# Lower triangles of 2048 Gram matrices on one core: laps of two tiles turned by halves, and stores of neighbouring batches as one run

## What is computed

```python
# inputs: (2048, 64, 256), float32
Z = jnp.einsum('bnd,bmd->bnm', inputs, inputs)
li, lj = jnp.tril_indices(64, k=-1)
y = Z[:, li, lj]
```

## Time and profile before

| | us |
|---|---|
| median of three runs (lowest to highest) | 401.72 (401.25 to 402.3) |
| the profiled execution, its own time | 403.43 |
| its span, first to last instruction | 401.6 |
| busy in the span: PE, DVE | 365.2, 362.3 |
| busy in the span: ACT, POOL | 178.4, 197.7 |
| DMA | 151.01 MB, 376 GB/s on average |

### The profile page before, as it was taken

How to read it: one execution, slowest core, us unless ns; L and a number is a source line. 1 busy time by engine, 2 the same in 40 slices (tenths; PEclk the granted TensorE clock), 3 DMA queues, 4 the chain that set the end, 5 groups by cost and what they waited for, 6 DMA issues and landing times.

```text
span 401.6 us, 68674 instructions
## 1 busy us (share of the span) xinstructions
PE 365.2 (91%) x33024; PEld 359.8 (90%) x33024; DVE 362.3 (90%) x240; ACT 178.4 (44%) x821; POOL 197.7 (49%) x974
## 2 busy tenths in 40 slices
PE   4439999999999999999999999998999899998960
PEld 4439999999999999999999999998989899998960
DVE  3417899999999999999999998989999798998995
ACT  0011224555445544465445654453554344455463
POOL 1000047282833866086817475283835738184585
PEclk9999999999999999999999999999999999999995
DMA  8299999999999999999999999999999999998417
GB/s 319 105 351 427 420 422 423 420 405 421 422 425 402 422 425 421 422 415 425 420 424 413 421 417 419 352 399 417 381 425 360 425 370 422 403 366 339 138 31 206
DMA packets 21274, 151.01 MB, mean 376 GB/s; under 512 B 2688, under 2 KB 2816, under 8 KB 4864
## 3 DMA queue, kind: packets, MB, share of 16 engines
q1 hardware_dynamic: 18752, 135.77, 83.8%
q10 hardware_dynamic: 2496, 14.97, 9.6%
HBM read 134.22 MB, written 16.52 MB: 375 GB/s over the span
## 4 chain that ended last, share of the span: by engine, by line
DVE 43%; DMA 34%; issue 13%; PE 8%; DVEq 0%
DVE x_turned L233 38%; DMA x_in<-x_dram 34%; PE bank_set L311 8%; DVE row_halves L250 3%; DVE x_in L257 1%; DVE packed_rows L153 1%; DVE packed_rows L142 0%; DVE x_turned L262 0%; DVEq L249 0%; DVEq L232 0%; DVEq L74 0%; DVEq L282 0%
## 5 line engine op out<-in xcount | busy, mean ns | idle before, releaser
L311 PE MATMUL bank_set<-x_turned 32*64 32x64 f32 x33024 | 365.2, 237 | 23.3 <-issue 15.1
L311 PEld LDWEIGHTS bank_set<-x_turned 32*64 32x64 f32 x33024 | 359.8, 132 | 28.5 <-issue 16.1
L233 DVE STREAM_TRANSPOSE x_turned<-x_in 128x2048 f32<-128x2048 f32 x128 | 287.9, 2280 | 33.8 <-PE bank_set L311 18.4
L153 POOL COPY packed_rows<-row_halves 32x32 f32<-32x32 f32 (+30 forms) x930 | 190.0, 204 | 198.3 <-DVE row_halves L250 98.6
L342 ACT COPY products<-bank_set 128x512 f32<-128x512 f32 (+1 forms) x91 | 68.4, 758 | 153.1 <-PE bank_set L311 141.0
L250 DVE STREAM_TRANSPOSE row_halves<-products 128x1024 f32<-128x1024 f32 x60 | 72.2, 1205 | 0.0
L142 ACT COPY packed_rows<-row_halves 128x32 f32<-128x32 f32 (+30 forms) x465 | 61.4, 220 | 16.6 <-DVE row_halves L250 16.5
L148 ACT COPY packed_rows<-row_halves 128x128 f32<-128x128 f32 x240 | 54.0, 299 | 27.8 <-DMA y_dram<-packed_rows 16.1
L342 ACT ACT_TABLE_LOAD x1 | 1.3, 1283 | 19.6 <-PE bank_set L311 19.6
L153 POOL COPY packed_rows<-x_in 32x32 f32<-32x32 f32 (+30 forms) x31 | 4.9, 209 | 0.1
L257 DVE STREAM_TRANSPOSE x_in<-products 128x512 f32<-128x512 f32 (+1 forms) x5 | 4.8, 998 | 0.0
## 6 DMA issues: line engine op xcount, KB each, us to landing
x_in<-x_dram SPq DMA_DIRECT2D x128, 1024.0 KB, 16.2
y_dram<-packed_rows ACTq DMA_DIRECT2D x22, 504.0 KB, 9.2
y_dram<-packed_rows ACTq DMA_DIRECT2D x6, 252.0 KB
y_dram<-packed_rows ACTq DMA_DIRECT2D x24, 63.0 KB
y_dram<-packed_rows SPq DMA_DIRECT2D x2, 504.0 KB, 4.7
y_dram<-packed_rows SPq DMA_DIRECT2D x1, 380.0 KB
y_dram<-packed_rows ACTq DMA_DIRECT2D x1, 380.0 KB
y_dram<-packed_rows SPq DMA_DIRECT2D x1, 124.0 KB
```

What stands on the lines that cost most here:

```text
L153: return copy(packed_rows[first:first + BLOCK, group % 2, :, at + BLOCK:at + i], halves(group)[first + BLOCK:first + HALF, i, :, 0:i - BLOCK])
L233: nc.vector.transpose(x_turned[:, j].rearrange("p c b s (h u n v) -> p u v (c b s h) n", h=ROWS // BLOCK, u=PAIRS, v=PAIR), x_in[:, k]).th ...
L311: done = nc.tensor.matmul(bank_sets[s][side * HALF:(side + 1) * HALF, g, at, :].rearrange("r (n u v) -> r u n v", u=PAIRS, v=PAIR), rows, ...
```

## The change

- The lap has two tiles instead of three, so 64 laps hold 128 tiles and the blank tile goes. x_turned has room for two tiles, and each PSUM set takes one.
- Each tile is turned and multiplied in two halves (PARTIALS), each of four of the eight chunks: DVE runs two transposes of 1024 elements a tile instead of one of 2048, with a semaphore for each place and half; PE waits for each half; a half's place is free once PE is done with that half. PE's order in a half is slot, then chunk; `start` is given once for a bank, at the first slot's first chunk.
- ACT keeps each tile by itself, 128 copies of 512 elements. They are written in another order, so that the two batches of a partition in packed_rows are neighbours in y: a run of 16128 bytes for each partition. For the last group the order stays as it was within each run, and SP and ACT store it in twice as many DMAs (HALF_SIDES), 16 partitions each.
- Small DMAs only in groups 1, 5 and 9 instead of 1, 3, 5, 7, 9 and 11: 12 instead of 24.
- Only load 4 is held, until PE is done with tile 0. Load 5 is not.
- PACK_LAG is 20 quarters instead of 19, counted against tiles instead of sets.

```diff
-    LAP = 3
-    LAPS = -(-TILES // LAP)
-    BLANK = LAPS * LAP - TILES
-    SET_TILES = (2, 1)
-    SETS = len(SET_TILES)
+    LAP = 2
+    LAPS = TILES // LAP
+    SETS = LAP
+    PARTIALS = 2
+    PARTIAL = CHUNKS // PARTIALS
...
-    PACK_LAG = 2 * PIECE_LAG - 3
+    PACK_LAG = 2 * PIECE_LAG - 2
...
+    HALF_SIDES = [[(side, q, q + BLOCK // SLOTS) for q in range(0, BLOCK, BLOCK // SLOTS)] for side in range(SIDES)]
...
-        x_turned = sbuf("x_turned", [PARTS, LAP, CHUNKS, SLOTS, SIDES, ROWS])
+        x_turned = sbuf("x_turned", [PARTS, LAP, CHUNKS, SIDES, SLOTS, ROWS])
...
+        def wait_kept(engine, t):
+            lap, s = place(t)
+            engine.wait_ge(kept[s], (lap + 2) * LAP)
...
         def by_few(group):
-            return group % 2 == 1 and group <= FEW_UNTIL
+            return group % 4 == 1 and group <= FEW_UNTIL
...
         def store(engine, group, columns, lanes):
-            rows = y[group * GROUP:(group + 1) * GROUP, columns].rearrange("(h q s) c -> s q h c", h=RUNS, s=SIDES)
+            rows = y[group * GROUP:(group + 1) * GROUP, columns]
             for side, first, end in lanes:
-                engine.dma_start(rows[side, first:end],
-                                 packed_rows[side * HALF + first:side * HALF + end, group % 2, :, columns]).then_inc(
-                    stored[group % 2], 16)
+                packed = packed_rows[side * HALF + first:side * HALF + end, group % 2, :, columns]
+                if group < GROUPS - 1:
+                    to = rows.rearrange("(q s h) c -> s q h c", s=SIDES, h=RUNS)[side, first:end]
+                else:
+                    to = rows.rearrange("(h q s b) c -> s b q h c", h=RUNS, s=SIDES, b=SLOTS)[side, first * SLOTS // BLOCK]
+                engine.dma_start(to, packed).then_inc(stored[group % 2], 16)
...
                 if t >= IN_RING:
                     lap, j = place(t - IN_RING)
-                    sync.wait_ge(turned[j], (lap + 1) * LAP)
+                    sync.wait_ge(turned[j][PARTIALS - 1], (lap + 1) * LAP)
                 elif t == LATE:
                     lap, j = place(0)
-                    sync.wait_ge(tile_multiplied[j], lap + 1)
-                elif t == LATE + 1:
-                    lap, j = place(0)
-                    sync.wait_ge(kept[set_of(j)[0]], (lap + 2) * LAP)
+                    sync.wait_ge(multiplied[j][PARTIALS - 1], lap + 1)
...
                 dve.wait_ge(loaded[k], (t // IN_RING + 1) * 16)
-                if lap > 0:
-                    dve.wait_ge(tile_multiplied[j], lap)
-                nc.vector.transpose(
-                    x_turned[:, j].rearrange("p c b s (h u n v) -> p u v (c b s h) n", h=ROWS // BLOCK, u=PAIRS, v=PAIR),
-                    x_in[:, k]).then_inc(turned[j], LAP)
+                for h in range(PARTIALS):
+                    chunks = slice(h * PARTIAL, (h + 1) * PARTIAL)
+                    if lap > 0:
+                        dve.wait_ge(multiplied[j][h], lap)
+                    nc.vector.transpose(
+                        x_turned[:, j, chunks].rearrange(
+                            "p c s b (h u n v) -> p u v (c s b h) n", h=ROWS // BLOCK, u=PAIRS, v=PAIR),
+                        x_in[:, k].rearrange("p (r d) -> p r d", r=JOINED)[
+                            :, :, chunks.start * BLOCK:chunks.stop * BLOCK]).then_inc(turned[j][h], LAP)
...
+                for h in range(PARTIALS):
+                    pe.wait_ge(turned[j][h], count)
+                    for slot in range(SLOTS):
+                        last_slot = h == PARTIALS - 1 and slot == SLOTS - 1
+                        if j == LAP - 1 and last_slot:
+                            pe.reg_add(count, count, LAP)
+                        for c in range(h * PARTIAL, (h + 1) * PARTIAL):
+                            if last_slot and c == CHUNKS - 2:
+                                pe.wait_ge(kept[1 - j], count)
...
+                                        start=c == 0 and slot == 0, stop=c == CHUNKS - 1 and slot == SLOTS - 1)
+                    done.then_inc(multiplied[j][h], 1)
...
+            def keep(t):
+                lap, s = place(t)
+                group, in_group = divmod(t, GROUP_TILES)
+                act.wait_ge(multiplied[s][PARTIALS - 1], lap + 1)
+                if group >= KEPT_RING and in_group == 0:
+                    act.wait_ge(rows_turned, (group - KEPT_RING + 1) * PIECES)
+                to = products[:, group % KEPT_RING]
+                if group < GROUPS - 1:
+                    to = to.rearrange("p i (b t g) -> p i t g b", b=RUNS, g=QUADRANTS)
+                else:
+                    to = to.rearrange("p i (r b t g) -> p r i t g b", r=RUNS, b=SLOTS, g=QUADRANTS)[
+                        :, in_group // (GROUP_TILES // RUNS)]
+                nc.scalar.copy(to[:, :, in_group % to.shape[2]], bank_sets[s][:, :, 0:SLOTS, :].rearrange("p g b i -> p i g b")).then_inc(
+                    kept[s], LAP)
...
-                    while n + PACK_LAG < (lap * LAP + (SET_TILES[0] if s == 0 else LAP) - BLANK) * 2:
+                while n + PACK_LAG < 2 * (t + 1):
```

More of the change, by code:

```diff
@@ L196, in _ @@
             for b in range(2):
-                last = 2 * len(WHOLE_SIDES) * 16 if (GROUPS - 1) % 2 == b else 0
+                last = 2 * sum(map(len, HALF_SIDES)) * 16 if (GROUPS - 1) % 2 == b else 0
                 sync.wait_ge(stored[b], stores_before(GROUPS + b) + last)
@@ L240, in turn_rows @@
                 if piece == 0:
-                    lap, j = place((group + 1) * GROUP_TILES - 1)
-                    s = set_of(j)[0]
-                    dve.wait_ge(kept[s], (lap + 2) * LAP)
+                    wait_kept(dve, (group + 1) * GROUP_TILES - 1)
                 if group > 0:
@@ L329, in _ @@
         def _(act):
-            def keep(lap, s):
-                j = SET_TILES[0] * s
-                act.wait_ge(tile_multiplied[j + SET_TILES[s] - 1], lap + 1)
-                begin = lap * LAP + j - BLANK
-                t, end = max(0, begin), begin + SET_TILES[s]
-                while t < end:
-                    group, in_group = divmod(t, GROUP_TILES)
-                    count = min(end - t, GROUP_TILES - in_group)
-                    if group >= KEPT_RING and in_group == 0:
-                        act.wait_ge(rows_turned, (group - KEPT_RING + 1) * PIECES)
-                    last = nc.scalar.copy(
-                        products[:, group % KEPT_RING, :, in_group * PER_SIDE:(in_group + count) * PER_SIDE].rearrange(
-                            "p i (m g b) -> p i m g b", g=QUADRANTS, b=SLOTS),
-                        bank_sets[s][:, :, (t - begin) * SLOTS:(t - begin + count) * SLOTS, :].rearrange(
-                            "p g (m b) i -> p i m g b", b=SLOTS))
-                    t += count
-                last.then_inc(kept[s], LAP)
+            def keep(t):
[12 more added lines that the diff above has]
+                    kept[s], LAP)
             def pack(n):
@@ L374, in _ @@
             few = 0
-            for lap in range(LAPS):
-                for s in range(SETS):
-                    keep(lap, s)
-                    if n >= (stores + 1) * PIECES * 4:
-                        store_whole(stores)
-                        stores += 1
-                        few = len(FEW_LANES) if by_few(stores - 1) else 0
-                    elif few > 0:
-                        store(act, stores - 1, slice(0, PACKED), FEW_LANES[-few:][:1])
-                        few -= 1
-                    while n + PACK_LAG < (lap * LAP + (SET_TILES[0] if s == 0 else LAP) - BLANK) * 2:
-                        pack(n)
-                        n += 1
+            for t in range(TILES):
+                keep(t)
+                if n >= (stores + 1) * PIECES * 4:
+                    store_whole(stores)
+                    stores += 1
+                    few = len(FEW_LANES) if by_few(stores - 1) else 0
+                elif few > 0:
+                    store(act, stores - 1, slice(0, PACKED), FEW_LANES[-few:][:1])
+                    few -= 1
+                while n + PACK_LAG < 2 * (t + 1):
+                    pack(n)
+                    n += 1
             for n in range(n, LAST_HOME):
```

47 lines of the change are left out of this document (14 added, 33 removed).

## The result

The changed kernel takes 409.17 us (median of 6 runs, 407.16 to 412.62) against 402.04 before (6 runs, 401.25 to 403.02): a ratio of 1.019, with a 95% interval of 1.014 to 1.024. The forecast was 394.7, with a range up to 400.0. The profiled execution took 407.16 us, its span is 405.4. One run of one kernel further down (the sevens) fell into a slower state of the chip, and its ratio and difference leave that run out.

What follows compares the result with a forecast made beforehand. PE and DVE were taken as equal bounds until about 240 us, then late loads. Start -3.7, load waits -9.5, pace +5.8, ends and rounding +0.4 gave 394.7 us, range 391.0 to 400.0.

Steps and rivals of the forecast that it cites:

- Fewer small stores: Stores, 12 small ones instead of 24: four engines' lag falls from 12 to 6 us, loads about 9.7 sooner with the start.
- the waits of 9.5 us: DVE's waits for loads after about 240 us: all go, -9.5 us, with 2 to 3 us to spare.
- near 4 of 16: End of the loads: a DMA share of 0.20 taken as four engines, those of the small stores, behind the rest.
- The start's gain: First lap: tile 0 ends and load 4 goes out one piece of code sooner, -3.7 us.
- the sum: Whole kernel: start -3.7, waits on loads -9.5, pace +5.8, ends and rounding +0.4; span 394.6 us, time 394.7.
- The first lap: Start: no blank tile and less code to wait for; load 4 and PE 3.7 us sooner, bounds 0 and 6.
- PE's pace: PE's laps: branching spread over two tiles instead of three, 2.76 becomes 2.79 us a tile.
- the turns by halves: DVE's transposes: two of 1024 add 0.055 us a tile; cycle 5.62 us for two tiles, DVE becomes the bound.
- A pair of batches as one run: Stores to y: same bytes, packets may double in size; at most 1.4 us, taken as 0.
- ACT: ACT's copies and issues: copies of 583 ns have room; four last-group DMAs instead of two cost +0.3 us on the path.
- the loads stay the bound: Rival, after 240 us: half of the 9.5 us stays, 399.5 us; if all, 404; chance 12%.
- dearer halves: Rival, DVE's turns: halves cost 131 ns a tile, not 55; cycle 5.77, time 403.4 us; chance 8%.

Runs made afterwards that it cites:

- the sevens: Kernel before, last 16 partitions of the second side stored as 7, 7 and 2 in nine groups: 18.1 us more, ratio 1.045.
- short stores: First 14 groups store only 128 of 2016 columns, rest of output left out: 393.07 us for the kernel before, 398.02 changed, against 402.77.
- eights: Kernel before, last 16 partitions of the second side stored as 8 and 8 in each of the first 14 groups: 426.04 us, ratio 1.060.
- sixes: Kernel before, last 16 partitions of the second side stored as 6, 6 and 4 in nine groups: 420.08 us, ratio 1.045.
- both parts taken back: Changed kernel with single runs, whole sides at the end and small stores in six groups again: 401.57 us against 401.88, ratio 0.9987.

## Why the prediction was wrong

The step that failed is *Fewer small stores*: "the lag of 12 us falls to 6. With the start, loads are about 9.7 us sooner at the end." The four engines did carry the small stores and did lag, by 8 us at the last load, and in the changed kernel this lag is gone. But they were not the last. One further engine was 3.8 us behind them, and the small stores were its relief: a group with them puts 6 runs on it instead of 8. With three such groups fewer it has 6 runs more, 3.2 us at 0.53 us each, and putting them back is worth 3.8 us. I read a share of 0.20 as "near 4 of 16" and did not ask who is last among those that are late; the stretch behind it, 377 to 380, held a store that hid it.

The same step had the waits of 9.5 us go. With short stores they do go, by 9.7 us, so their size and their cause in transfers were right. In the real run 7.7 of them stay in the window of the earlier trace rows and one more of 1.35 us stands before the last tile. The start's gain was not lost on PE: load 4 landed at 20.2 us instead of 24.5. It was the slow engine's chain that did not become shorter. From load 4 to load 127 it takes 363.5 us instead of 356.2. It had 14 runs more to store before its last load, 7.4 us at 0.53 each. Six of them, 3.2 us, come from the fewer small stores. The other eight, 4.2 us, are one whole store: the one issued at 373.26 now lies among that engine's loads (its last two loads landed 6.7 us apart), while the one at 377.51 before came when it was nearly done (2.5 apart). So the whole gain of the start went into a store that now comes before the last load, which the sum had at nothing.

Point by point:

- *The first lap*: right in kind, too small. The last piece of code came 5.6 us sooner and load 4 landed 4.3 us sooner, not 3.7.
- *PE's pace* and *the turns by halves*: right. DVE's cycle is 5.63 against 5.62; ACT's copies, which follow PE, stand 5.61 us apart for two tiles. The small fixed cost (0.055 us a tile) held, not the 131 ns.
- *A pair of batches as one run*: the packets did become 16128 bytes, of 601 ns where two took 610, and the gain is nothing, as taken. But the step left out what the layout does to ACT's copy: its time nearly doubled. It lay beside other work, as far as the runs show: taking back layout and ends gave 3.7 us, of which the ends are 2.3; 1.4 us are left for the copies and the packets, within what the runs scatter, and the last load did not land sooner without them (384.8 against 383.7).
- *ACT*, the ends: the term of +0.3 was mis-sized. Twice as many DMAs cost 2.3 us, because the third issue of the last group takes 2.4 us on both queues, not 0.4. Why it does is open.
- The net of the terms other than loads: the changed kernel with short stores has a span of 394.9 us, where the sum said 394.6; part of that nearness is luck, since the start gained more and the ends cost more.

Of the rivals the second, "the loads stay the bound", was right, with 12%, and its time of 404 was still too low, since it had no loss by the stores and none at the ends. The one on the slower side that I had priced, dearer halves, did not happen. The range took in half of that rival only, and left no room for a term with the sign turned.

In short: +3.8 from fewer small stores, +2.3 from the halved ends, about +1.4 left over for the layout (not shown), and nothing from the rest, make 7.5 us, where 7.1 were measured.

## What to carry to other kernels

Where transfers end late, find out who is last, engine by engine, before pricing a relief; a share of 4/16 that fades to 1/16 is two different causes, and a change that helps the four can load the one. An odd-looking piece of a tuned kernel, here small DMAs in some groups, may be a balance between two chains within a few per cent: price it from both sides. A chain that is not the last one may change for nothing, however right its price: here the dearer DVE cycle vanished under the loads' chain. And when a start comes sooner, look at what else moves with it: here a store slid in among the last loads and took the gain again.

## What the runs showed of the hardware

- One DMA engine of sixteen is slower in stores from SBUF to DRAM: 0.53 us for each run of 8 KB by its landings, against 0.305 by the packets of the others, and 0.53 to 0.83 us of the kernel's time for each further run. Most load packets, its own among them, take 309 ns. With loads and stores in one queue it lags too. It is no fault of one chip: the experiments ran on four, and on each one engine lands the last load far behind the next (388.9 against 378.1 us without small stores, 402.8 against 389.4 with eights, 393.5 against 379.1 with stores on SP, 397.4 against 386.2 with sixes). What makes it slow is open.
- ACT's copy of 512 elements from PSUM took 583 ns with eight neighbouring elements written in a row, and 1096 ns when each next element lay about 128 bytes away. The Trainium skill, SBUF — State Buffer, section "Door 1: The DMA port swizzle", says that SBUF is accessed in lines of 16 bytes and that each crossing to a new line costs; the two durations agree with that.
- The third of the last group's four DMAs of 16 partitions took 2.44 us to issue on both queues, where the first two took 0.33 to 0.37 and 0.43 to 0.45. It did so in all four traces with halved ends (2.38 to 2.45 us). It is no matter of the third alone: with only the ends halved, the second of a whole store's two DMAs took 2.37 us at 377.0. Why is open.
- The changed kernel's runs scatter over 5.5 us, those of before over 1.8. Why was not tried.

No version beat the kernel before: the changed one with both parts taken back equals it.
